# Decoder layer on one core: feed-forward weights measured among the slots, rounded in one VectorE pass, head 0 prepared before the border

## What is computed

```python
x = _layernorm(x + attn(x))          # norm, W_in, short filter, long convolution, gate, W_out
x = _layernorm(x + xattn(ctx, x))    # 32 heads of 8: k_i * v_j, causal convolution with ssm_kernel, times q_i
x = _layernorm(x + ffn(x))
def _bitlinear(x, w):
    rms = jax.lax.rsqrt(jnp.maximum(jnp.mean(w * w), EPS))
    w_quant = jnp.clip(jnp.round(w * rms), -1.0, 1.0) / rms
    scale = 127.0 / jnp.maximum(jnp.max(jnp.abs(x), axis=-1, keepdims=True), EPS)
    x_quant = jnp.clip(jnp.round(x * scale), -128.0, 127.0) / scale
    return jnp.einsum('bsd,fd->bsf', x_quant, w_quant)
# ffn: _bitlinear(gelu(_bitlinear(x, w1)), w2), w1 (2048, 512), w2 (512, 2048)
```

## Time and profile before

| | |
|---|---|
| median of 3 runs | 1130.29 us (1128.77 to 1130.85) |
| the profiled execution | 1128.79 us, its span 1127.0 us |
| PE busy | 1052.1 us (93%) |
| DVE, ACT, POOL busy | 816.0, 589.4, 586.0 us |
| granted TensorE clock, mean | 0.977 |
| second half: slots | about 262 to 400 us of the span |
| second half: output stage | 400 to 479 us |
| border, start of the heads | 479 to 517 us |
| heads, PE full | 517 us on |

### The profile page before, as it was taken

The page is one execution under the profiler, slowest core; times in us unless marked ns, Lnnn a source line. Parts: engine busy times, 40 slices in busy tenths (PEclk is TensorE's granted clock), DMA queues, the critical chain, the costliest instruction groups (busy, mean ns, idle before and its releaser), DMA issues.

```text
span 1127.0 us, 16879 instructions
## 1 busy us (share of the span) xinstructions
PE 1052.1 (93%) x5316; PEld 643.6 (57%) x5316; DVE 816.0 (72%) x1531; ACT 589.4 (52%) x710; POOL 586.0 (52%) x1136
## 2 busy tenths in 40 slices
PE   1799899999999987969999999999999999999985
PEld 1455455544545533556676767676766666666652
DVE  6978786696565546857777878787878787777762
ACT  2355444203444463825565656565656565666654
POOL 2301310131000003559878787878787878788770
PEclk9899899999999998989999999999999999999997
DMA  8233445455244584332121222212131313131101
GB/s 236 93 89 113 146 140 172 147 177 177 92 133 150 150 328 147 122 112 58 57 84 58 74 67 65 74 57 83 50 89 47 93 47 93 47 90 50 47 10 29
DMA packets 95215, 115.23 MB, mean 102 GB/s; under 512 B 19584, under 2 KB 52352, under 8 KB 93632
## 3 DMA queue, kind: packets, MB, share of 16 engines
q1 hardware_dynamic: 95168, 114.63, 33.5%
HBM read 80.90 MB, written 33.70 MB: 102 GB/s over the span
## 4 chain that ended last, share of the span: by engine, by line
PE 53%; POOL 2%; ACT 1%; DVE 1%; issue 0%; POOLq 0%; DVEq 0%
PE conv_bank L1255 26%; PE hq_bank L1289 10%; PE ff_bank L1317 5%; PE back_bank L1317 5%; PE ctx_bank L1230 1%; PE ff_bank L1282 1%; PE hq_bank L1282 1%; PE back_bank L1240 1%; PE back_bank L1269 1%; PE ctx_bank L1300 1%; POOL up L1626 0%; POOL dn L1627 0%; POOL up L1629 0%; ACT o L1415 0%; POOL att L1639 0%
## 5 line engine op out<-in xcount | busy, mean ns | idle before, releaser
L752 DVE SCALAR_TENSOR_TENSOR conv_all<-u,taps,conv_all 128x1024 f32<-128x1024 f32 x96 | 126.4, 1317 | 97.9 <-ACT conv_all L624 96.1
L1255 PE MATMUL conv_bank<-block_diag 128*128 128x288 f32 x640 | 175.6, 415 | 8.8 <-PEq L265 6.0
L1255 PE MATMUL conv_bank<-kv,block_diag 128*128 128x288 f32 x640 | 171.7, 408 | 0.0
L938 POOL TENSOR_SCALAR r_rstd<-r_meanvar 128x1 f32<-128x1 f32 x32 | 13.0, 407 | 258.3 <-DVE r_meanvar L776 258.3
L616 ACT ACTIVATE u<-slot_bank,bias,unscale 128x1024 f32<-128x1024 f32 x48 | 57.9, 1207 | 164.9 <-PE slot_bank L466 161.3
L1255 PEld LDWEIGHTS conv_bank<-block_diag 128*128 128x128 f32 x640 | 120.1, 194 | 40.6 <-issue 6.6
L1626 POOL TENSOR_TENSOR up<-z_up 128x384 f32<-128x384 f32 x128 | 127.7, 998 | 27.9 <-DVE z_dn L1502 27.0
L1255 PEld LDWEIGHTS conv_bank<-kv,block_diag 128*128 128x128 f32 x640 | 117.8, 190 | 30.9 <-DVE z_dn L1502 0.5
L1490 DVE TENSOR_TENSOR z_up<-conv_bank,qx 128x512 f32<-128x512 f32 x128 | 87.7, 685 | 55.6 <-PE conv_bank L1255 43.3
L1557 DVE TENSOR_REDUCE g_max<-g 128x1 f32<-128x512 f32 x128 | 87.3, 683 | 54.8 <-ACT g L1430 54.8
L1289 PE MATMUL hq_bank<-x_lo,hq_t 128*128 128x512 f16 x512 | 124.6, 388 | 1.6 <-ACT hq_t L1397 1.6
(11 more groups left out here) (175 smaller groups left out, 1880.5 us busy)
## 6 DMA issues: line engine op xcount, KB each, us to landing
v_scratch<-conv_all SPq DMA_DIRECT2D x16, 512.0 KB, 2.9
c_scratch<-v_tok SPq DMA_DIRECT2D x8, 1024.0 KB, 4.5
y<-c_scratch SPq DMA_DIRECT2D x8, 1024.0 KB, 4.8
res<-in_x SPq DMA_DIRECT2D x32, 256.0 KB, 2.9
x_scratch<-res SPq DMA_DIRECT2D x32, 256.0 KB, 2.0
block_diag<-in_ctx SPq DMA_DIRECT2D x32, 256.0 KB, 3.4
block_diag<-ssm_scratch SPq DMA_DIRECT2D x32, 256.0 KB, 3.1
x_tok<-x_scratch SPq DMA_DIRECT2D x32, 256.0 KB, 3.7
```

The costliest lines, as they stand in the source:

```text
L752: ins = nc.vector.scalar_tensor_tensor(out=acc, in0=u[:, t0 + tap:t0 + tap + T // 2, :].rearrange("p t b -> p (t b)"), scalar=w["taps"][:, ...
L1255: last = nc.tensor.matmul(view(conv_bank[tb % 2][:, hh, :], 0, (ROW64, T // 2), (1, PAIRS)), toep[:, head.buf, (tb - sb_) * P:(tb - sb_ + ...
```

## The change

1. The squares get loads of their own, `load_stat`, into the two `x_quad` tiles in turn, and `square` is done on ACT behind eight of the slots of the second half. Sum, mean and power follow in slots 18 to 21. The weights are then loaded a second time for rounding (`load_part`), in part earlier than before.
2. Rounding: ACT does `round_part` in place (times rms plus a constant whose low f16 half holds the rounded value), DVE one clamp (`clip_part`), PE transposes the low halves, and ACT's copies subtract a constant. `make_ternary` is gone. Parts 0 and 1 are rounded behind slots 21 and 23. `turn_part` now stands behind rows 1 to 8 instead of 7 to 14.
3. Head 0: x1 of heads 0 and 1 is loaded before the first row of the stage; the context is transposed behind row 11, the products stand behind row 12 on DVE, and the first two row blocks of head 0's convolution stand behind the last row. In the heads, x1's transpose comes first.
4. Residual rows are loaded three ahead instead of two, in both halves.

```diff
+        SQUARE_AT = {1: 0, 3: 1, 5: 2, 8: 3, 10: 4, 12: 5, 15: 6, 17: 7}
+        TOTAL_AT, SUM_MATRIX_AT, MEAN_AT, INVERSE_AT = 18, 19, 20, 21
+        ROUND_AT = {21: 0, 23: 1}
+        CLIP_AT = {i - 1: i for i in range(2, 2 * PARTS)}
+        PART_AT = {1 + i: i for i in range(2 * PARTS)}
+        CTX_AT, PAIRS_AT = 11, 12
...
+                def load_stat(i):
                     if i < 2:
                         sp.wait_ge(x_turned, DC * (HALF * NQ - 1 + i))
+                    else:
+                        sp.wait_ge(squared, i - 1)
+                    sp.dma_start(part_target(i, part_raw[i % 2]), part_source(i)).then_inc(stat_loaded[i % 2], 16)
...
                     if hf + 1 == HALF:
+                        load_stat(0)
+                        load_stat(1)
+                        regroup(hf, 0)
+                        load_stat(2)
+                        load_stat(3)
+                        load_stat(4)
+                        bring_back(hf, 0)
+                        load_stat(5)
+                        regroup(hf, 1)
+                        load_stat(6)
+                        load_stat(7)
+                        bring_back(hf, 1)
+                        regroup(hf, 2)
                         load_part(0)
                         load_part(1)
+                        bring_back(hf, 2)
+                        regroup(hf, 3)
+                        load_part(2)
+                        load_part(3)
+                        bring_back(hf, 3)
+                        for i in range(4, 2 * PARTS - 1):
                             load_part(i)
...
+                        for h in range(2):
+                            heads = slice(h * HD, (h + 1) * HD)
...
+                            sp.dma_start(early["x1_tok"][:, h, :], dram["x1_scratch"][:, heads, :]).then_inc(early["x1_loaded"][h], 16)
                     for t in range(T):
                         R = hf * T + t
-                        if R + 2 < HALF * T:
-                            load_res(R + 2)
+                        if R + 3 < HALF * T:
+                            load_res(R + 3)
                         store_res(R)
...
+                def convolve_first(tb):
+                    if tb == 0:
+                        pe.wait_ge(early["toep_loaded"][0], 16)
+                        pe.wait_ge(early["kv_done"], 1)
+                        pe.wait_ge(part_done, 2 * 2 * PARTS)
...
+                            elif cc == DC - 1:
+                                pe.wait_ge(mean_made, 1)
                             convolve(hf, cc, others, quad)
...
                 def square(i):
+                    act.wait_ge(stat_loaded[i % 2], 16 * (i // 2 + 1))
+                    nc.scalar.activation(part_raw[i % 2], part_raw[i % 2], ACT.Square,
+                                         accum_out=sums[:, i // PARTS, i % PARTS:i % PARTS + 1]).then_inc(squared, 1)
+                def round_part(i):
...
+                    nc.scalar.activation(part_raw[i], part_raw[i], ACT.Copy, scale=rms[:, m:m + 1], bias=LOW_HALF).then_inc(rounded, 1)
...
-                        nc.scalar.copy(out, src).then_inc(part_done, 1)
+                        nc.scalar.activation(out, src, ACT.Copy, bias=-HALF_ONE).then_inc(part_done, 1)
...
+                def clip_part(i):
+                    dve.wait_ge(rounded, i + 1)
+                    nc.vector.tensor_scalar(part_raw[i], part_raw[i], LOW_HALF - 1.0, LOW_HALF + 1.0, ALU.max, ALU.min).then_inc(clipped, 1)
...
                 def convolve(head, tb, blocks):
+                    if head.c == 0 and tb < 2:
+                        return
...
                 def body(n):
                     h1, h2 = n.back(1), n.back(2)
+                    if n.c == 0:
+                        turn_x1(n)
```

More of the change, by code:

```diff
@@ L31 @@
 TOEP = P + L
+ROW64 = 64
 EPS = 1e-5
@@ L184, in hyena_block @@
         taps_ready = sem("taps_ready")
+        stat_loaded = [sem(f"stat_loaded{i}") for i in range(2)]
         part_loaded = [sem(f"part_loaded{i}") for i in range(2 * PARTS)]
@@ L395, in _ @@
                 load_res(1)
+                load_res(2)
                 bring_back(0, 2)
@@ L1015, in toeplitz, with first_conv @@
     return bass.AP(src.tensor, h * TOEP + 1, [[1, P], [1, L]])
+def first_conv(nc, early, bank, tb, sb_, hh):
+    half = T // 2
+    return nc.tensor.matmul(view(bank, 0, (ROW64, half), (1, PAIRS)), early["toep"][:, 0, (tb - sb_) * P:(tb - sb_ + 1) * P],
+                            early["kv"][:, sb_ * T + hh * half:sb_ * T + (hh + 1) * half, :], start=(sb_ == 0), stop=(sb_ == tb))
 def reverse_blocks(nc, early, buf):
```

219 lines of the change are left out of this document (105 added, 114 removed).

## The result

The changed kernel takes 1116.2 us (median of 4 runs, 1114.8 to 1116.9) against 1130.6 of the kernel before (4 runs): 0.9877 of it, interval 0.9865 to 0.989. It is faster by 14.4 us. The forecast was 1105 with a range from 1101.5 to 1111, so the direction was right and the size was not, and the time lies outside the range.

A forecast was written before the change was run, and what follows sets the result against it. PE bounds the slots and heads; between them it waits for a reduction behind late rows, then DVE paces rows at 4.43 us. 15.2 - 0.1 + 8.3 + 0.8 = 24.2 us less gives 1105 us, range 1101.5 to 1111.

The forecast's parts named there:

- Output stage, 15.2: Second half: last output matmul (X) at 463.5 for 478.67, DVE one pass less, PE setting 4.33 us rows; 15.2 us less.
- "Cost 0" in the slots: Second half's slots: squarings fit ACT's idle time and SP's extra loads delay nothing; cost 0, plus 0.1 for a matmul.
- number 2: Squaring behind slot 5, the only one without slack: ACT starts slot 6 at 302.1, PE needs it at 306.6; cost 0.
- Later a store has a whole row, 4.33 us, to land: Output stage, rows after row 4: loads waiting for an earlier row's store would find it landed, with 4.33 us for it.
- a gain of 0.8: First half: one more residual row loaded ahead removes DVE's waits and PE's idle time; 0.8 us, between 0 and 0.84.
- Start of the heads, 8.3: Last output matmul (X) to DVE's first product of head 0: X + 6.15 against X + 14.5, 8.3 us less.
- late rows: First rival, second output stage: residual rows still land late behind weights, PE idles 5.3 us; 1110 to 1111, chance 0.15.
- Loads in the slots: Third rival, second half's slots: squarings wait for their loads, six losing 1 to 3 us each; 1110 to 1122, chance 0.06.
- the prediction's price (what exceeds 3.66): Slots: a squaring waiting for its load delays ACT's next slot; PE pays what exceeds 2.88 + 2.88 - 2.1 = 3.66 us.
- The border gives little: Second rival, start of heads: something unmoved holds head 0, gain 2.2 us for 8.3; 1111 to 1112, chance 0.07.
- The signs of being wrong: PE waiting for weight clamps or slot banks, squarings and PE waiting for loads, or POOL's first addition after X + 9 us.
- The table loads that the prediction weighs: ACT in the slots: squaring in another function set would bring 16 loads, 43 us, and a slower kernel; trace decides for none.

The follow-up runs named there:

- e10: e5 with DVE's clamp made twice, the second changing nothing: 1107.3 us, 0.9796 of the kernel before.
- e12: e1 with spare tiles putting nine large tiles, also x_quad, x_hi, x_lo, block_diag and res, on multiples of 512 bytes: 1105.8 us, 0.9797 of the kernel before.
- e17: e1 with nine unused tiles, large tiles 256 bytes beyond a multiple of 512: 1106.0 us, 0.9797 of the kernel before.
- e18: The kernel of e12 run again: 1107.1 us, 0.9815 of the kernel before.
- e5: e1 plus one unused 4-byte tile where minus_round stood, large tiles back on multiples of 512 bytes: 1108.6 us, 0.9817 of the kernel before.
- e16: e5 with head 0's first twelve convolution passes behind the border again: 1109.7 us, 0.9799 of the kernel before.
- e9: The changed kernel run again, unchanged: 1115.3 us, 0.986 of the kernel before.
- e1: The changed kernel with SP issuing the store of row R before the load of row R + 3: 1108.2 us, 0.9811 of the kernel before.
- e14: The kernel of e1 run again: 1108.6 us, 0.9794 of the kernel before.
- e2: The changed kernel with residual rows loaded two ahead again, load before store: 1113.5 us, 0.9854 of the kernel before.

## Why the prediction was wrong, step by step

The shortfall is 24.2 - 12.4 = 11.8 us of span. By the first table: start 3.1, first output stage 1.5, slots 3.5, second output stage 0.3, border 2.7, remainder 0.6. About 5.7 of it (1.5, 1.5 of the slots, 2.7) is SP's serial loop, 1.9 the tiles' places, and 3.1 stays open.

- **Output stage, 15.2: right.** 14.95 measured; the one pause was at part 2, as predicted, 0.36 for 0.5. The reason given for DVE (one pass less) was not what carried it, by e10, and a row with transposes takes PE 4.38 us for the 4.33 of the prediction. In the kernel before the late rows took 4.38 as well (469.90 to 474.28), so the rows themselves gave next to nothing.
- **"Cost 0" in the slots: wrong by 3.5.** 1.5 us is squaring 0. The prediction gives number 2 alone as without slack; that holds for loads issued at 266 us, where the weight loads stood before, but load 0 stands behind the last rows of the first half on SP, whose loop was slower: 275.97. The walk through SP's queue left out its first entry. About 1.9 us are tile addresses. Without both, in e10 to e12, e17 and e18, the slots take 138.7 us (138.9 in e5 and e16): the predicted 0.1. Squaring 2, which I had picked as the tight one, waited 7.15 us and cost PE nothing.
- **"Later a store has a whole row, 4.33 us, to land": the step that failed.** The load of row R + 3 waits for the store of row R - 1, but that store is itself issued only after the load before it has been released, so it has what is left of the round, not a row. I had written that the next store is queued behind that wait, and drew the consequence for rows 3 and 4 only. It cost 2.7 us at the border, 0.75 in the first output stage where I had booked a gain of 0.8, and the late squaring. With the store first both terms are as predicted: 61.9 to 62.3 us, and X + 6.1. One profile is out of line: in e16 the first output stage takes 63.9 us, with a pause whose cause is open (its code is that of e5 there):

```profile
239.37 1.97 PE L476 MATMUL conv_bank<-ident,x_quad 128*128 128x128 f32 x16 [1.79 <-DVE x_quad L775]
```

- **Start of the heads, 8.3: right in itself,** 8.35 with the store first, 5.6 in the changed kernel.
- **What no step had:** 3.1 us ahead of the first output matmul, where the change adds one load of a residual row. PE pauses 0.45 us for a convolution there. The addresses don't explain that: e5, with its tiles on the boundary, pauses 0.54 us at this place and e12 1.61, e17 and e18 not at all. The rest is TensorE's clock and small shifts in one execution. In e9 that stage is 200.5, and over the other profiles it lies between 197.5 and 202.1 us, so much of the 3.1 was bad luck.

```profile
191.47 3.81 PE L516 MATMUL conv_bank<-v_ct,block_diag 128*128 128x128 f32 x32 [0.54 <-issue]
```


Of the rivals, *late rows* did not stop PE in the second output stage. *Loads in the slots* came for one squaring of eight: number 0 waited 5.29 us, for which the prediction's price (what exceeds 3.66) gives 1.6, and PE paused 1.51. Its cause was not the rival's, since the 8 MB cost 0.2 us, but the late issue on SP. That rival's times (1110 to 1122, chance 0.06) hold the result, but with one squaring late instead of six they hold it by chance. *The border gives little* came in part: X + 8.9 for 6.2. The wait behind most of it, on SP for a landing, was in none of them. The signs of being wrong did come: PE waited for a slot bank behind a squaring, and POOL's first addition stands at 481.58, X + 10.4, for the 9 that the prediction allowed.

The table loads that the prediction weighs did not come: between 3 and 506 us ACT has none, and squaring 1 starts at 289.87 as the pass before it ends. The price put on them was too high as well: two of 2.7 us per squaring would by the prediction's own 3.66 cost PE 1.7 us each time, 14 in all, which makes the change smaller and not slower than before.

## What to carry to other kernels

Prefetching one buffer further ahead changes which store a load waits for; write down for every wait in a queue when the transfer it waits for was issued, and what stands between. If it is the one just issued, the loop is serial, and its period (landing and issue) is to be set against the consumer's. Put the store first: here that gave 7 to 8 us (1116.2 to 1108.2, and 1115.3 to 1108.6), of which 5.9 can be read from the stages.

A tile added or removed moves all that are allocated behind it. Compare the landings of transfers that a change did not touch before explaining waits by what it did touch.

## What the runs showed of the hardware

- SBUF addresses: the same strided transfer of 512-byte pieces lands 13% later (5.1 for 4.5 us) with its tile off a 256-byte boundary, at offsets of 480, 64 and 128 bytes alike (table above).
- A store of 256 KB lands after 2.0 us when the load of the same size is issued behind it, and after 3.2 us when the load is issued 0.4 us ahead of it (medians of e1 and of the changed kernel; 2.0 also in the kernel before, where the load goes out a row earlier).
- TensorE's clock near the start differs between executions: the same 8 matmuls took 2.05 us in e1 and 3.60 in e14, which are one kernel. They took 2.00 us before and 3.60 us after, with a granted clock of 0.97 and 0.50 (windows: from, to, us, busy us of PE alone or of all five engines, clock, DMA share, GB/s; first before, then after). The second is the lower of the two levels, 1.2 GHz; in both PE had worked in bursts with pauses of 3.2 to 4.3 us from 29 us until then. A pause of 11.6 us in the kernel before (0.53 behind it) and one of 3.2 us in e2 (0.50 behind it) show the same.

```profile
50.25:54.00 3.75, 3.75 (x17) 0.97 0.00 0
```

```profile
50.60:54.00 3.40, 3.40 (x9) 1.20 (x10) 3.35 (x5) 0.00 (x0) 0.00 (x0) 0.50 0.00 0
```
